# Ahead of the first block: own buffers for three key and query splits and an earlier store, value pieces in the maximum banks, bias sums in steps between the chunks

## The reference

```python
a = _layer_norm(ctx, gamma, beta)                 # layer 0
x = x + tanh(gate) * (softmax(x@Wq.T . (a@Wk.T)) (a@Wv.T)) @ Wo.T
h = layer_norm(x, ln1_w, ln1_b)                   # layer 1, its keys and values from ctx itself
q, k, v = h@q_w + q_b, ctx@k_w + k_b, ctx@v_w + v_b
x = softmax(q . k) v @ cproj_w + cproj_b + x
y = gelu(layer_norm(x, ln2_w, ln2_b) @ fc_w + fc_b) @ proj_w + proj_b
return x + y
```

## Time and profile before

| | us |
|---|---|
| Median of 3 runs | 2037.35 (2036.52 to 2040.63) |
| Profiled execution, its own time | 2044.37 |
| Span of the profiled execution | 2042.5 |
| Mean granted TensorE clock, share of full | 0.981 |
| TensorE busy in the span | 1960.1 (96%) |
| First score matmul of block 0 starts at | 98.04 |

### The profile page before, as it was taken

The page is one execution under the profiler, slowest core; times in us unless marked ns, Lnnn a source line. Parts: engine busy times, 40 slices in busy tenths (PEclk is TensorE's granted clock), DMA queues, the critical chain, the costliest instruction groups (busy, mean ns, idle before and its releaser), DMA issues.

```text
span 2042.5 us, 38305 instructions
## 1 busy us (share of the span) xinstructions
PE 1960.1 (96%) x14940; PEld 1053.3 (52%) x14940; DVE 1417.5 (69%) x2389; ACT 1298.0 (64%) x2327; POOL 424.1 (21%) x441
## 2 busy tenths in 40 slices
PE   5899999999999999999999999999999999999996
PEld 4345545455554545555554555545555554554544
DVE  3677777767677776777767676686767777676742
ACT  2166656667666675667756676666766667665773
POOL 2041113103141132311232022310323103111110
PEclk8799989999999999999999999999999999999998
DMA  6435152341515242251522515143241525214100
GB/s 150 126 83 150 45 140 54 97 107 58 123 43 129 68 126 60 54 150 37 138 63 71 130 35 149 41 112 92 79 102 51 129 60 139 63 37 114 30 7 6
DMA packets 142698, 176.01 MB, mean 86 GB/s; under 512 B 35092, under 2 KB 113085, under 8 KB 140469
## 3 DMA queue, kind: packets, MB, share of 16 engines
q1 hardware_dynamic: 140373, 170.67, 32.0%
q10 hardware_dynamic: 2144, 2.90, 0.6%
HBM read 125.33 MB, written 48.16 MB: 85 GB/s over the span
## 4 chain that ended last, share of the span: by engine, by line
PE 76%; DVE 6%; SPq 5%; ACT 5%; DMA 4%; POOL 3%; issue 2%; ACTq 0%
PE p_sc L1114 18%; PE p_acc L1147 18%; PE p_mx L1134 14%; PE p_misc L1182 9%; PE p_misc L1175 6%; DMA scr_k<-parts 3%; PE p_misc L1220 2%; PE p_misc L1208 2%; PE p_misc L1168 2%; DVE maxes L869 2%; SPq L499 2%; SPq L486 2%; PE p_misc L1214 2%; ACT prob L779 2%; DVE rest L949 2%
## 5 line engine op out<-in xcount | busy, mean ns | idle before, releaser
L869 DVE TENSOR_REDUCE maxes<-p_mx 128x1 f32<-128x802 f32 x1024 | 985.7, 984 | 336.1 <-PE p_mx L1134 332.1
L779 ACT ACTIVATE prob<-p_sc 128x512 f32<-128x512 f32 (+1 forms) x1664 | 963.1, 596 | 328.7 <-PE p_sc L1114 326.7
L1114 PE MATMUL p_sc<-qst,kst 100*128 100x256 bf16 (+1 forms) x3328 | 647.3, 276 | 23.3 <-ACT prob L779 22.1
L1134 PE MATMUL p_mx<-kst,qst 97*128 97x401 bf16 x2048 | 528.0, 339 | 10.1 <-DVE maxes L869 9.2
L1147 PE MATMUL p_acc<-prob,vals 128*17 128x256 f32 x6656 | 523.1, 386 | 0.2
L1114 PEld LDWEIGHTS p_sc<-qst,kst 100*128 100x128 bf16 (+1 forms) x3328 | 262.0, 99 | 505.5 <-ACT prob L779 215.1
L622 POOL TENSOR_TENSOR parts<-rest,parts 128x512 bf16<-128x512 f32 (+1 forms) x144 | 139.7, 970 | 638.5 <-DVE parts L960 638.4
L1147 PEld LDWEIGHTS p_acc<-prob,vals 128*17 128x17 f32 x6656 | 110.4, 95 | 243.4 <-issue 195.2
L1134 PEld LDWEIGHTS p_mx<-kst,qst 97*128 97x128 bf16 x2048 | 192.9, 99 | 54.3 <-DVE maxes L869 26.3
L1182 PE MATMUL p_misc<-wv,ctxt 128*128 128x256 f32 x800 | 193.5, 383 | 2.0 <-DVE rest L949 2.0
L1175 PE MATMUL p_misc<-ctxt,wk 128*128 128x512 f32 x488 | 191.1, 514 | 1.4 <-ACT vals L733 0.7
(11 more groups left out here) (143 smaller groups left out, 1084.3 us busy)
## 6 DMA issues: line engine op xcount, KB each, us to landing
kst<-scr_k SPq DMA_DIRECT2D x384, 200.1 KB
scr_k<-parts SPq DMA_DIRECT2D x96, 384.0 KB, 3.1
ctxn<-in_ctx_dram SPq DMA_DIRECT2D x16, 1536.0 KB
qst<-scr_q SPq DMA_DIRECT2D x384, 32.0 KB, 2.9
scr_q<-parts SPq DMA_DIRECT2D x16, 384.0 KB, 3.1
xin<-in_x_dram SPq DMA_DIRECT2D x8, 256.0 KB, 2.8
out_dram<-y SPq DMA_DIRECT2D x8, 256.0 KB, 2.0
scr_k<-parts SPq DMA_DIRECT2D x32, 48.8 KB, 2.3
```

Of the source, the lines that this page charges most:

```text
L779: act.activation(prob[0:rows, u % 2, 2 * half:2 * half + 2, :].rearrange("p h t -> p (h t)"), p_sc[0:rows, half, :], ACT.Exp).then_inc(exp ...
L869: dve.tensor_reduce(maxes[:, c:c + 1], p_mx[:, c % 2, :, 0:CW], AX.XY, ALU.max).then_inc(chunk_done, 1)
L1114: ins = mm(p_sc[0:rows, half, T * q:T * q + T], kst[0:RB, h, P * j:P * j + rows], qst[0:RB, h, :], start=True, stop=True)
L1134: ins = mm(p_mx[:, c % 2, w, 0:CW], qst[0:RA, h, P * t:P * t + P], kst[0:RA, h, s0:s0 + CW], start=True, stop=True)
```

## The change

Four things are changed, all in block -1 or just behind it. (1) The splits of K 0 2, K 0 3 and Q get buffers of their own, in `prob`, `g_t`, `o_t` and `x1`, which hold nothing yet; so they no longer wait for stores of earlier splits. K 0 3's split waits for the mask store, because the mask lies in `g_t`. (2) SP stores these keys right after the mask has been stored; the value bias is stored after `fetch_queries` of group 0, and spread after the stores of K 1 0 and K 1 1. The next context's load moves from behind K 1 1 to behind the maxima. (3) The seven value pieces leave `FIRST`: they stand together behind Q, and use the four banks `p_mx`. (4) `second_setup` is cut into 14 steps, one behind each chunk from the third to the sixteenth (2 products with one column each, then 2 with one row each); DVE reads the sums behind MX (`read_shifts`), and folds the weights of layer 1 at unit 8 of block 0.

The diff, cut:

```diff
 FIRST = ([("XT",)] + [("T", k) for k in range(7)] + [("K", 0, c) for c in range(4)]
-         + [("Q",), ("V", 0), ("V", 1), ("V", 2), ("V", 3), ("V", 4), ("K", 1, 0), ("K", 1, 1), ("MX", NG), ("V", 5),
-            ("K", 1, 2), ("K", 1, 3), ("V", 6)])
-FIRST_CHUNKS = {("MX", NG): range(16), ("V", 5): range(16, 18), ("K", 1, 2): range(18, 20),
-                ("K", 1, 3): range(20, 21), ("V", 6): range(21, 16 + EARLY)}
+         + [("Q",), ("K", 1, 0), ("K", 1, 1), ("MX", NG), ("K", 1, 2), ("K", 1, 3)])
+FIRST_VALUES_AFTER = ("Q",)
+FIRST_CHUNKS = {("MX", NG): range(16), ("K", 1, 2): range(16, 19), ("K", 1, 3): range(19, 16 + EARLY)}
+SETUP_FROM, SETUP_STEPS = 2, 14
...
-        return self.n0 >= 0 or o >= 2
+        return self.n0 >= 0 or o >= 5
...
+        def split_space(blk, o):
+            if blk.n0 >= 0 or o not in (2, 3, 4):
+                buf = blk.split_buffer(o)
+                return parts[buf], rest[:, buf, :]
+            if o < 4:
+                own = (prob[:, 0, :, :] if o == 2 else g_t[:, 0:4, :]).rearrange("p h t -> p (h t)")
+                left = (prob[:, 1, :, :] if o == 2 else g_t[:, 4:8, :]).rearrange("p h t -> p (h t)")
+            else:
+                own = o_t[:, :, :].rearrange("p g t -> p (g t)")
+                left = x1[:, :, :].rearrange("p t d -> p (t d)")
+            return own[:, 0:768].bitcast(BF16).rearrange("p (k c) -> p k c", k=3), left[:, 0:512]
...
-            sp.wait_ge(bias_saved, 3)
-            sp.wait_ge(const_made, 10)
-            with nc.allow_non_contiguous_dma(reason="a vector from columns, once"):
-                sp.dma_start(scr_vb.rearrange("(c p) -> p c", p=P), cols[:, 39:41]).then_inc(vb_moved, 16)
+            sp.wait_ge(mask_stored, 16)
+            def store_value_bias():
+                sp.wait_ge(bias_saved, 3)
+                with nc.allow_non_contiguous_dma(reason="a vector from columns, once"):
+                    sp.dma_start(scr_vb.rearrange("(c p) -> p c", p=P), cols[:, 39:41]).then_inc(vb_moved, 16)
+            def spread_value_bias():
                 sp.wait_ge(vb_moved, 16)
-                for q in range(HG):
-                    sp.dma_start(vb_pad[0][32 * q:32 * q + DH, :],
-                                 scr_vb.rearrange("(g q d) -> q d g", q=HG, d=DH)[q]).then_inc(vb_moved, 16)
-            sp.wait_ge(mask_stored, 16)
+                with nc.allow_non_contiguous_dma(reason="a bias spread over the heads' rows, once"):
+                    for q in range(HG):
+                        sp.dma_start(vb_pad[0][32 * q:32 * q + DH, :],
+                                     scr_vb.rearrange("(g q d) -> q d g", q=HG, d=DH)[q]).then_inc(vb_moved, 16)
...
-                    if blk.n0 < 14 and (u == CTX_LOAD_AT[blk.par] if blk.attends else piece == ("K", 1, 1)):
+                    if blk.n0 < 14 and (u == CTX_LOAD_AT[blk.par] if blk.attends else kind == "MX"):
...
                     if blk.n0 < 0 and piece == ("Q",):
                         fetch_queries(blk, 0)
+                        store_value_bias()
+                    if blk.n0 < 0 and piece == ("K", 1, 1):
+                        spread_value_bias()
                         fetch_keys(n + 1, blk, 1, blk.prep_b, True)
...
-                    buf = blk.split_buffer(o)
+                    buf, (ps, _) = blk.split_buffer(o), split_space(blk, o)
                     if blk.split_ever(o):
                         act.wait_ge(parts_out[buf], 16 * blk.split_uses(o))
-                    act.activation(parts[buf][:, 0, 0:w], res[:, 0:w], ACT.Identity,
+                    elif o == 3:
+                        act.wait_ge(mask_stored, 16)
+                    act.activation(ps[:, 0, 0:w], res[:, 0:w], ACT.Identity,
                                    bias=kbias[blk.prep][:, piece[1]:piece[1] + 1]).then_inc(high_ready, 1)
...
+                    if blk.n0 < 0 and piece == FIRST_VALUES_AFTER:
+                        for k in range(NT // 2 + 1):
+                            act.wait_ge(first_values, k + 1)
+                            js = tile_pair(k)
+                            rows = tile_rows(js[0])
+                            act.activation(vals[0][0:rows, js[0]:js[-1] + 1, :, 0:DH],
+                                           p_mx[0:rows, k // 2 % 2, k % 2, 0:D * len(js)].rearrange(
+                                               "p (j h d) -> p j h d", j=len(js), h=H),
+                                           ACT.Copy).then_inc(first_values_saved, 1)
...
+                dve.wait_ge(row_summed, 1)
+                dve.tensor_copy(bias_row[:, 0, :], p_sc[0:1, 0, 0:D]).then_inc(row_saved, 1)
+                dve.tensor_tensor(bias_row[:, 1, :], p_sc[0:1, 1, 0:D], hid[0:1, 0, :], ALU.add
+                                  ).then_inc(row_saved, 1)
+            def fold_second():
...
+                        if blk.n0 < 0 and piece[0] == "MX":
+                            read_shifts()
+                    if blk.n0 == 0 and u == 8:
                         fold_second()
...
+            def second_setup(step):
+                if step == 0:
+                    pe.wait_ge(misc_saved, make_block(-1, 0).misc(("MX", NG)))
+                    pe.wait_ge(loaded, LOADED)
+                if step < CH + FT:
+                    w, shift, col, m = (wq[1], c_b1, 0, step) if step < CH else (wfc, c_b2, CH, step - CH)
+                    for c in range(CH):
+                        ins = mm(p_acc[:, T + col + m:T + col + m + 1], w[:, c, P * m:P * m + P], shift[:, c:c + 1],
+                                 start=(c == 0), stop=(c == CH - 1))
+                    if step == CH + FT - 1:
+                        ins.then_inc(bias_summed, 1)
+                    return
+                if step == CH + FT:
+                    pe.wait_ge(vb_moved, 16 * 5)
+                    pe.wait_ge(w_saved, 5)
+                l, k = (step - CH - FT) // 2, step % 2
+                for g in (2 * k, 2 * k + 1):
+                    ins = mm(p_sc[0:1, l, 0:D], vb_pad[l][:, g:g + 1], wo[l][:, g, :],
+                             start=(g == 0), stop=(g == NG - 1))
+                if step == SETUP_STEPS - 1:
+                    ins.then_inc(row_summed, 1)
+            def first_value_tiles(blk, k):
+                if k == 0:
+                    pe.wait_ge(w_saved, 5)
+                if k >= 4:
+                    pe.wait_ge(first_values_saved, k - 3)
+                for j in tile_pair(k):
+                    r, o = tile_rows(j), D * (j % 2)
+                    for c in range(CH):
+                        ins = mm(p_mx[0:r, k // 2 % 2, k % 2, o:o + D], ctxt[:, j, c, 0:r], wv[blk.prep][:, c, :],
+                                 start=(c == 0), stop=(c == CH - 1))
+                ins.then_inc(first_values, 1)
...
+                            if g == NG and c >= SETUP_FROM:
+                                second_setup(c - SETUP_FROM)
+                        if blk.n0 < 0 and piece == ("K", 1, 2):
+                            pe.wait_ge(row_saved, 2)
                         do_piece(blk, piece)
-                        if blk.n0 < 0 and piece == ("Q",):
-                            second_setup()
+                        if blk.n0 < 0 and piece == FIRST_VALUES_AFTER:
+                            for k in range(NT // 2 + 1):
+                                first_value_tiles(blk, k)
             walk(visit)
```

More of the change, by code:

```diff
@@ L335, in build @@
         max_in = sem("max_in")
+        first_values = sem("first_values")
+        first_values_saved = sem("first_values_saved")
         misc_ready = sem("misc_ready")
@@ L618, in split_low @@
                 o = split_no(piece)
-                s, buf = blk.split(o), blk.split_buffer(o)
+                s, (ps, left) = blk.split(o), split_space(blk, o)
                 w = chunk_cols(piece[2]) if piece[0] == "K" else 512
                 pool.wait_ge(mid_ready, s + 1)
-                pool.tensor_tensor(parts[buf][:, 2, 0:w], rest[:, buf, 0:w], parts[buf][:, 1, 0:w], ALU.subtract
+                pool.tensor_tensor(ps[:, 2, 0:w], left[:, 0:w], ps[:, 1, 0:w], ALU.subtract
                                    ).then_inc(low_ready, 1)
@@ L846, in fold_first, with read_shifts @@
                     dve.tensor_scalar(wq[0][:, c, :], wq[0][:, c, :], scale, None, ALU.mult).then_inc(folded, 1)
-            def fold_second():
+            def read_shifts():
                 dve.wait_ge(loaded, LOADED)
@@ L948, in do_piece @@
                     if kind == "K":
-                        dve.scalar_tensor_tensor(out=rest[:, buf, 0:w], in0=res[:, 0:w], scalar=bias,
-                                                 in1=parts[buf][:, 0, 0:w], op0=ALU.add, op1=ALU.subtract
+                        dve.scalar_tensor_tensor(out=left[:, 0:w], in0=res[:, 0:w], scalar=bias,
+                                                 in1=ps[:, 0, 0:w], op0=ALU.add, op1=ALU.subtract
                                                  ).then_inc(misc_saved, 1)
@@ L954, in do_piece @@
```

(20 more changed lines are left out.)

20 lines of the change are left out of this document (8 added, 12 removed).

## The result

Over 20 runs of each the changed kernel takes 2033.76 us (2029.44 to 2037.54) and the kernel before 2038.38 (2036.23 to 2043.04): ratio 0.9975, 95% interval 0.9967 to 0.9982. By the ratio that is 5.1 us less (0.0025 x 2038.38), by the two medians 4.6. The forecast was 2034.4 in a range of 2030.0 to 2041.0. The profiled execution after took 2035.96 us (span 2034.1). Three single executions stand in no comparison: one of before (2699.89 us), one of e4 (4673.41) and e2, the first execution of e2b's kernel (4673.99; four of its key products take 5.05 us instead of 1.98, at a recorded clock of 1.00).

A forecast was written before the change was run, and what follows sets the result against it. SP's chain of stores and PE's chain were taken to reach the first chunk together at 67.0, then DVE paces. -10.0 + 7.2 - 0.1 = -2.9 us, from the median 2037.35 to 2034.4; range 2030.0 to 2041.0.

The forecast's parts named there:

- The mask and SP's chain: Block 0's setup: without the bias store the mask lands by 36, splits bind, first chunk at 57.0, 10.0 us earlier.
- The first rival, a late mask: SP's first key store: mask lands as late as before, store at 40.9, total 2039.0 us; chance 0.23.
- PE's chain: PE before the first chunk: no longer binds, K 1 1 done at 52.4, then idles 4.6 us.
- The loop: Sixteen chunks with steps between: half clock, PE paces instead of DVE, 24.6 us, 7.2 more than before.
- a pair of chunk and step is thus 1.5 us: Chunk loop at half clock: chunk 0.65 plus step 0.87, over DVE's 0.96; ten pairs 15.0 us.
- The 7.4 for the last four pairs: Loop's end, chunks with one-row steps: two pairs of 2.4 us at clock 0.50, two of 1.3 at 1.00.
- the pairs cost more: Chunk loop rival: pairs of 1.65 or 1.75 us, all row steps at 0.50, total 2039.9 us; chance 0.10.
- the full clock: Chunk loop rival: clock stays 1.00, pairs 0.9 us under DVE's 0.96, total 2025.2 us; chance 0.09.
- The tail: From the last maximum to block 0's first scores: 13.6 us, 0.1 less than before.
- within 0.2%: Whole kernel: time differs from before by under 0.2% (4 us); chance 0.65, against 0.26 faster and 0.09 slower.
- The bias store behind the queries: Rival at group 0's query fetches: slow writes hold their last landings up to 4.6 us, total 2039.1; chance 0.10.
- What was costed at nothing: Weight folding in block 0's unit 8 (2 us if uncovered), later context load, later group fetches: no time added.

The follow-up runs named there:

- e4: Changed kernel with the bias stored and spread before the key stores and the three splits in the shared buffers again; ratio to before 1.0026.
- e2: First execution of the changed kernel with the bias store right behind the mask store, spread late; 4673.99 us, in no comparison.
- e2b: Changed kernel with the bias store right behind the mask store, spread late; no ratio, one execution, block 0's start shifted -0.3 us against before.
- e1: Changed kernel with the value bias stored and spread before the first key store; ratio to before 1.0012.
- e6: Changed kernel with twelve unread products of 256 columns filling PE's idle time behind K 1 1; ratio to before 0.9964.
- e5: Changed kernel with the ten one-column steps moved from between the chunks into PE's idle time behind K 1 1; ratio to before 0.9964.
- e8: Changed kernel with the one-column steps behind K 1 1 and the bias stored as 128 writes of eight bytes; 2030.11 us, ratio to before 0.9956.
- e3: Changed kernel with the splits of K 0 2, K 0 3 and Q in the shared buffers again; ratio to before 0.9991.
- e9: The changed kernel itself, repeated in a later batch; 2034.82 us, ratio to before 0.9974.
- e7: Changed kernel with the bias stored and spread first, as 128 writes of eight bytes; no ratio, block 0's start shifted 0.0 us against before.

## Why the prediction was nearly right, point by point

**The mask and SP's chain: right.** "The mask is in by about 36 once it is gone": e1 shows a landing 8.5 us after the issue, which is 34.8 for a mask issued at 26.34, and e2b shows that the bias store is the cause of the other 6 us. The splits bind, as said. The low part of K 0 2 ends at 39.56, 6.6 us behind the first key copy (forecast 6.9); from there it is 4.2 us to the key fetch (3.7) and 14.3 on to the first chunk (14.4). Forecast for the stretch 24.95, measured 25.14. The first rival, a late mask, is out. One argument in that rival's favour was misread, though: PE's wait that ended at 40.73 was given as a landing behind the slow writes, but that load was issued at 26.00, ahead of the bias store. So the trace of before may already hold a sign of what e2b shows, which the rule named there doesn't cover.

**PE's chain: right.** PE was done with K 1 1 at 53.2 (52.4 forecast, in an execution that began 0.9 later) and then idled 4.9 us for the queries (4.6).

**The loop: mechanism right, one term mis-sized.** Clock 0.50, PE without idle time, third chunk at +1.92 (1.9), and from the thirteenth chunk to the last maximum's end 7.6 us (7.4 - 0.9 + 1.2 = 7.7). The term that failed is "a pair of chunk and step is thus 1.5 us": it took 1.34. The chunk was entered at 0.65 from the start of its neighbour, the step at 0.87 from a stretch of one-column products alone. Laid alternately the step adds only 0.72 (60.65 to 61.37) to the chunk's 0.64 (60.01 to 60.65), and slightly less in the later pairs. Why four of them are cheaper than in a row of their own wasn't tested. Ten pairs make 1.6 us, over half of the error. The 7.4 for the last four pairs took half of them at each clock level, a choice for which no row stood. It came out: these pairs take 2.57, 2.08 and 1.40 us, the fourth about as long as the third, with the clock at 0.87 from 77 to 79 and 1.00 behind that. That much was luck. The rival "the pairs cost more" is out, and so is the full clock; in e6, where the loop began with it, the same pairs lost it.

The Trainium skill (TensorE: Matmul & The Clock Gate, What's actually happening) says "the default state is throttled, and activity releases the throttle". For a PE that was merely busy the trace doesn't bear it out: at 62 to 65.4 it was busy for 3.40 of 3.40 us, at 0.50, and in e5 and e6 the clock fell to 0.50 under it.

**The tail: 1.0 us shorter than forecast.** K 1 2 could start 4.2 us after the last maximum (4.6) and took 3.1 (3.5, all at half clock); behind it 5.3 instead of 5.5.

**The sum.** Forecast -2.9; with +0.2 at the first chunk, -1.7 in the loop and -1.0 in the tail that is -5.4, and the table has -5.3, the ratio -5.1, the medians -4.6. The forecast's 2034.4 came closer to the measured 2033.76 than these terms deserve, by luck: the kernel before measured 1.0 us higher in the 20 runs than in the three that I started from. The chances followed the sum: with -2.9 "within 0.2%" had to be likeliest, and with 1.6 us of slack in one term it was too sure of it. The result, 0.25%, lies just beyond that bound, and its interval (0.18 to 0.33%) reaches across it.

**The bias store behind the queries: the rival is out, its mechanism isn't.** The last query fetch is issued at 55.9 and the first chunk starts at 58.09: not held. But what stands behind the bias store is. The DMA table and two stretches of the changed kernel, 56 to 66 us (the first: KB each, median us from issue to landing):

```profile
scr_k<-parts SPq DMA_DIRECT2D x2, 384.0 KB, 12.6
...
scr_vb<-cols SPq DMA_DIRECT2D x1, 1.0 KB, 9.0
```

```profile
58.00:60.00 2.00, 1.50 (x4) 0.43 (x4) 1.04 (x2) 0.00 (x0) 0.00 (x0) 0.50 2.09 216
60.00:62.00 2.00, 1.99 (x9) 1.62 (x10) 1.84 (x2) 0.00 (x0) 0.00 (x0) 0.50 0.72 6
```

The stores of K 1 0 and K 1 1 take 12.6 us, where those of the first keys take 4.6 and 3.8 in the same trace, and the traffic falls from 216 to 6 GB/s. The same two stores take 4.2 us in e1, where the bias store is long in, and 6.6 in e8, where it stands beside them in pairs. The change moved this cost to a place where nothing waited for it; e5 made PE fast enough to meet it.

**What was costed at nothing: one of the terms has a price.** The context load was issued at 84.26, and DVE's statistics began at 95.86 without a wait on it. PE waited for no query fetch in block 0 up to 160. But the folding of weights in block 0's unit 8, at DVE 111.7 to 113.9, lies beside POOL's first context tiles, and those set the pace there: POOL's 13 tiles take 16.39 us instead of 15.70, and PE's first wait for one ends 3.3 us behind their start instead of 2.6, so all of the 0.7 falls into that stretch. They take 16.4 in the traces of e1, e2b and e3 to e9 too, which all have the folding there. That the folding is the cause is argued from this and wasn't tested on its own.

## What to carry to other kernels

When a chain waits for a store, look at what small writes to DRAM stand near it in the queues, behind it as well as ahead: here 256 of them cost other transfers 6 us. Widen such a store first, then move it off the chain. Small products that have to go somewhere belong where TensorE idles, not between chunks that another engine paces; and each time a stretch is made faster, read what will now be waited for in it.

## What the runs showed of the hardware, unexpected

- A store of 256 writes of four bytes to DRAM lands in 7.8 us with the queues nearly empty (e1) and 9.0 us with traffic (changed kernel); one of 128 writes of eight bytes in 3.1 (e7) and 3.3 (e8). While the first is under way, large transfers beside it take some three times as long (12.6 us for 384 KB, against 4.2 in e1).
- A landing can be late because of a store issued after it (14.5 us in e2b against 8.5 in e1 for the mask).
- TensorE's clock fell from 1.00 to 0.50 under a busy engine: in e5 at 56 to 57.7 us, without a gap since 37.90 and with one-column products alone since 52.56; in e6 at about 63.4 us, with these and chunks in turn (busy 3.73 of 3.90 us).
- POOL's 13 context tiles took 16.4 us with DVE's weight folding beside the first of them and 15.7 without it.
